# Transposing the gated output by a DMA transfer instead of by TensorE and a ScalarE copy

## What is computed

```
rk = normalise(x per head);  wk = rk one step later;  v = x Wv^T
gate = sigmoid(x Wg^T);  beta = sigmoid(x Wb^T)
for t:  err = (v_t - wk_t S) * beta_t;  S += wk_t err^T;  o_t = (rk_t S) * gate_t
attn = o Wo^T
x = x + layernorm(attn(layernorm(x)))
x = x + layernorm(ffn(layernorm(x)))       # ffn: inputs clipped, weights rounded to -1, 0, 1
```

## Time and profile before

| | |
|---|---|
| median of 3 runs | 2561.44 us (2545.59 to 2561.95) |
| profiled execution | 2552.82 us, span 2551.1 us |
| PE busy | 2161.4 us (85%) |
| PE weight loads busy | 1350.0 us (53%) |
| DVE busy | 2239.5 us (88%) |
| ACT busy | 1699.0 us (67%) |
| POOL busy | 1731.3 us (68%) |
| mean granted TensorE clock | 0.947 of full |
| DMA | 215.50 MB, mean 84 GB/s |

### The profile page before, as it was taken

The page is one execution under the profiler, slowest core; times in us unless marked ns, Lnnn a source line. Parts: engine busy times, 40 slices in busy tenths (PEclk is TensorE's granted clock), DMA queues, the critical chain, the costliest instruction groups (busy, mean ns, idle before and its releaser), DMA issues. The chain is left out here.

```text
span 2551.1 us, 146840 instructions
## 1 busy us (share of the span) xinstructions
PE 2161.4 (85%) x61989; PEld 1350.0 (53%) x61989; DVE 2239.5 (88%) x6603; ACT 1699.0 (67%) x3372; POOL 1731.3 (68%) x2841
## 2 busy tenths in 40 slices
PE   1679999999999999999999989999998747777776
PEld 1356555556555565555655555556655524434442
DVE  4599999999999999999999999999999837777875
ACT  2667777777777777777777777777774335555554
POOL 1556777767777776777777767776775335777777
PEclk7789999999999999999999999999999868888888
DMA  2112222222222222222222222222222124565554
GB/s 79 51 46 63 71 79 76 75 71 72 78 72 78 72 75 72 75 78 71 75 76 78 72 71 78 77 74 71 73 66 62 53 95 146 152 162 153 153 139 99
DMA packets 132137, 215.50 MB, mean 84 GB/s; under 512 B 31352, under 2 KB 31360, under 8 KB 131488
## 3 DMA queue, kind: packets, MB, share of 16 engines
q1 hardware_dynamic: 131488, 206.20, 28.4%
HBM read 104.40 MB, written 67.11 MB: 67 GB/s over the span
## 5 line engine op out<-in xcount | busy, mean ns | idle before, releaser
L740 DVE TENSOR_TENSOR ps_elim<-ps_elim,sys 128x30 f32<-128x30 f32 (+14 forms) x1920 | 543.4, 326 | 0.8
L748 DVE TENSOR_TENSOR sys<-sys,ps_elim 128x30 f32<-128x30 f32 (+14 forms) x1920 | 534.4, 316 | 1.0
L893 PE MATMUL ps_v<-wv,xt 128*128 128x512 f16 x1536 | 433.5, 391 | 34.7 <-DMA kbd<-kt 20.5
L893 PE MATMUL ps_y<-wo,ot 128*128 128x512 f16 x1536 | 404.3, 387 | 12.4 <-DVE x L811 10.1
L1293 PE MATMUL ps_f<-wq,f_xq 128*128 128x512 f16 x1024 | 281.6, 426 | 102.1 <-ACT f_yn L1169 97.5
L920 PEld LDWEIGHTS ps_chain<-rhs,t_t 32*32 32x32 f32 x16384 | 263.1, 144 | 127.0 <-issue 121.7
L543 POOL TENSOR_TENSOR o_g<-pred,gate 128x512 f32<-128x512 f32 x128 | 134.3, 1049 | 286.1 <-DVE pred L827 286.1
L920 PE MATMUL ps_chain<-rhs,t_t 32*32 32x32 f32 x16384 | 294.5, 218 | 20.2 <-issue 12.8
L620 ACT ACTIVATE z<-x,z_sc 128x512 f32<-128x512 f32 x128 | 104.1, 814 | 265.4 <-POOL z_sc L519 265.4
L528 POOL TENSOR_TENSOR m_t<-gram,b_mask 128x512 f32<-128x512 f32 x128 | 164.3, 1283 | 147.7 <-ACT gram L627 141.7
L914 PEld LDWEIGHTS ps_chain<-state,key_t 32*32 32x32 f32 x16384 | 174.5, 105 | 158.2 <-issue 156.4
(11 more groups left out here) (155 smaller groups left out, 5157.7 us busy)
## 6 DMA issues: line engine op xcount, KB each, us to landing
x_in<-in_L_attn_x SPq DMA_DIRECT2D x128, 256.0 KB
kbd<-kt SPq DMA_DIRECT2D x512, 64.0 KB
x_res<-in_L_attn_x SPq DMA_DIRECT2D x128, 256.0 KB
x_scratch<-x SPq DMA_DIRECT2D x128, 256.0 KB, 6.4
f_x<-x_scratch SPq DMA_DIRECT2D x32, 1024.0 KB, 7.6
out<-f_res SPq DMA_DIRECT2D x128, 256.0 KB, 3.9
gate<-gates SPq DMA_DIRECT2D x128, 7.9 KB
gate<-gates SPq DMA_DIRECT2D x128, 0.2 KB
```

Of the source, the lines that this page charges most:

```text
L740: dve.tensor_tensor(tmp, factors(r, c, first, end)[:, c - first:C - 1 - first, c - first:c - first + 1].to_broadcast(shape), sys[:, r, c:c ...
L748: dve.tensor_tensor(dst, dst, tmp, ALU.add).then_inc(elim_done[r], 1)
L893: last = pe.matmul(out, lhs[:, a, kb, :], weights[:, w, kb, :], start=(i == 0), stop=(i == 3 * KB - 1))
```

## The change

PE's transposes and ACT's copy of `ot` are taken out, and with them the bank `ps_ot` and the semaphores `ot_psum` and `ot_done`. SP issues one transposing transfer per tile instead, from `o_part` to `ot`, between the load of `x_res` and the store of `x1`; it waits for `olo_done` of this tile and for the output matmuls of the tile two before. Whoever waited for the transposes (ACT and POOL before they write `o_part`) or for the copy (PE before the output) now waits for the transfer's semaphore, one per buffer.

```diff
+        OT = 16
+        ot_loaded = [sem(f"ot_loaded{i}") for i in range(2)]
@@ SP's step, after the load of x_res
+                n, l, live = on(base, j, LAG_OUT)
+                if live:
+                    wait(sp, s["olo_done"], n + 1)
+                    wait(sp, s["y_psum"], n - 1)
+                    sp.dma_start_transpose(ot[:, l % 2, :, :, :].rearrange("p a k t -> p (a k) t"),
+                                           o_part[:, l % 2, :, :].rearrange("p a n -> p (a n)")).then_inc(ot_loaded[l % 2], 16)
@@ POOL, LAG_PART (before L534), and ACT, LAG_PART (before L601)
-                    wait(pool, s["ot_psum"], n - 1)
+                    wait(pool, ot_loaded[l % 2], halves(base, j, LAG_PART) * OT)
-                    wait(act, s["ot_psum"], n - 1)
+                    wait(act, ot_loaded[l % 2], halves(base, j, LAG_PART) * OT)
@@ ACT, LAG_OUT
-                    wait(act, s["ot_psum"], n + 1)
-                    wait(act, s["y_psum"], n - 1)
-                    nc.scalar.activation(ot[:, l % 2, :, :, :].rearrange("p a k t -> p (a k t)"), ps_ot[:, :].bitcast(F16),
-                                         ACT.Copy).then_inc(s["ot_done"], 1)
@@ PE, LAG_OUT
-                    wait(pe, s["ot_done"], n)
-                    wait(pe, s["olo_done"], n + 1)
-                    for a in range(2):
-                        for kb in range(KB):
-                            last = pe.transpose(ps_ot[:, :].bitcast(F16)[:, D * a + P * kb:D * a + P * kb + P],
-                                                o_part[:, l % 2, a, P * kb:P * kb + P], k["ident_half"][:, :])
-                    last.then_inc(s["ot_psum"], 1)
@@ PE, before the output matmuls
-                    wait(pe, s["ot_done"], y + 1)
+                    wait(pe, ot_loaded[y_l % 2], halves(base, j, LAG_Y) * OT + OT)
```

More of the change, by code:

```diff
@@ L314, in attention @@
         ps_elim = [bank(f"ps_elim{i}") for i in range(2)]
-        ps_ot, ps_v = bank("ps_ot"), bank("ps_v")
+        ps_v = bank("ps_v")
         ps_gram, ps_chain, ps_s, ps_y = bank("ps_gram"), bank("ps_chain"), bank("ps_s"), bank("ps_y")
@@ L336, in attention @@
             pred_psum rhs_done err_psum err_done s_psum state_done
-            pred_done o_done ohi_done olo_done ot_psum ot_done y_psum
+            pred_done o_done ohi_done olo_done y_psum
             y_var y_veps y_rstd x1_done
@@ L640, in step @@
                     nc.scalar.activation(err[:, :], ps_chain[:, :], ACT.Copy).then_inc(s["err_done"], 1)
-                n, l, live = on(base, j, LAG_OUT)
-                if live:
-                    wait(act, s["ot_psum"], n + 1)
-                    wait(act, s["y_psum"], n - 1)
-                    nc.scalar.activation(ot[:, l % 2, :, :, :].rearrange("p a k t -> p (a k t)"), ps_ot[:, :].bitcast(F16),
-                                         ACT.Copy).then_inc(s["ot_done"], 1)
                 n, l, live = on(base, j, LAG_TURN)
```

## The result

The changed kernel takes 2894.74 us at the median (2877.94 to 2912.13, 4 runs) against 2561.69 us: 1.1315 times as long, interval 1.1232 to 1.1398. The forecast was 2605 us, the range 2505 to 2800. The profiled execution took 2898.19 us, its span is 2896.5 us.

A forecast was written before the change was run, and what follows sets the result against it. DVE was taken as today's bound, PE close behind; with the change SP's chain, 12.78 + 2.46 + 0.25 = 15.49 us, 0.34 over today's step: +41 us in 119 steps, +44 with the end, forecast 2605 us, range 2505 to 2800.

The forecast's parts named there:

- What bounds the kernel: In the long stretch, DVE is the bound with 14.6 us of work in a 15.15 us step, PE right behind.
- SP's chain: SyncE's queue: 12.78 us a step with 2.37 us of slack, growing to 15.49 us with the change.
- the sign of a wrong mechanism: In SP's timeline: SP waiting for kt 1 us or more a step while the kernel is still slower.
- The issue on SP: On SP's queue: one transposing issue a tile, taken as 2.46 us, between 0.61 and 4.9 us.
- The wait for the gates: On SP, the gate transfer behind the new one: 0.25 us more a step, between 0 and 1.15 us.
- The engines' work: On the DMA engines: 0.9 us for each 256 KB, with 2.5 us of issuing giving them time to drain.
- the cost that had no term: On PE: only the removal was counted, at best ending DVE's wait for PE, 0.42 us a step.
- a way to be wrong: On PE: its "issue" waits might grow with the traffic; no size was given.
- The landing: Transfer's arrival in ot: 5.5 us after its issue starts, 0.1 to 0.35 us past DVE's limits.
- Rival 3: DVE stalls in L779 behind ACT's L601 because of a late landing of 6.4 us: 2615 to 2645 us, chance 0.12.
- Rival 2: On SP, the eight blocks are paid one by one, 4.9 us of issue: about 2895 us, chance 0.21.
- Rival 1: SP's slack swallows the issue and freed PE and ACT time shows: about 2525 us, chance 0.27.

The follow-up runs named there:

- the swap: The changed kernel with the transposing transfer and the load of x_res exchanged in SP's order, so it stands right behind kbd: 2589.84 us, ratio 1.0092.
- e6_early: The changed kernel with the transposing transfer moved up in SP's order, in front of kbd: 2593.32 us, ratio 1.0072.
- e2_three: The changed kernel with three buffers of o_part instead of two: 2869.64 us, ratio 1.1237 to the kernel before.
- e12_removed: The changed kernel without any transfer in place of PE's transposes and ACT's copy, ot staying zero: 2564.87 us, ratio 1.0046 to the kernel before.
- e3b_plain_three: The changed kernel with a plain transfer of the same bytes instead of the transposing one, and three buffers of o_part: 2566.65 us, ratio 0.9984.
- e1_beside: The kernel before plus a transposing transfer of the same size to a spare tile, for which only SP waits: 2972.26 us, ratio 1.1644.

## Why the prediction was wrong, step by step

**What bounds the kernel: right.** DVE with PE behind it, and SP's chain with 2.4 us of slack; the swap, which uses the slack up, shows that chain as the bound (0.16 us of wait for `kt` left). There the forecast's mechanism holds, and its time is near, 2605 against 2589.84 us. In the change itself it does not: SP waits 3.0 us a step for `kt`, which the prediction had named as the sign of a wrong mechanism.

**The issue on SP: overstated.** 2.46 us was taken; the median is 1.29 us in the change and 1.27 in the swap, the mean 1.55 and 1.64. Some of the rest came back in other issues: in the swap SP issues for 7.6 us a step in all against 5.5 before. The time hardly depends on size: 1.24 us (median) for half the columns. By the 32 cycles a tile of the Trainium skill's page "DMA: Bandwidth & Descriptors", in its table of sequencer time, half the columns should have cost half; the rows do not agree. The wait for the gates, for which 0.25 us was added, is 6.8 us a step, as before.

**The engines' work: the step that failed.** "so 0.9 us for each 256 KB", and "2.5 us of issuing gives the engines time to drain". A plain transfer's price was put on the transposing one, and nothing was asked about the load ahead of it. By the DMA share the engines' work has grown from 3.9 us a step to 9.1 (0.50 x 18.1), by 5.1 us; by 2.1 us in `e6_early`, where nothing is in front (0.39 x 15.5), and by 0.7 us with the plain transfer (0.30 x 15.6), for which the prediction's price is about right. From first to last packet it lasts 5.07 us, 1.7 where nothing is in front.

**PE: the cost that had no term.** The sum had only gains on PE. That its issue waits could grow with traffic stood last, as a way to be wrong. They grew by 2.3 us a step. They were in the profile before, 0.85 us a step, up to 1.5 us long; asking what feeds the instruction stream would have led to the DMA queue.

**The landing: right in kind, small in size.** 5.5 us was taken, 6.8 is the median. Rival 3's chain, `L601` to `L779`, is in the trace at 1.5 us a step, but it does not add to the starvation: `e2_three` takes it away, and the ratio only goes from 1.1315 to 1.1237.

**Rival 2 has the number by luck.** It gave 2895 us for an issue of 4.9 us. The issue is under a third of that, and SP waits for others. The Trainium skill's page "VectorE: DVE Perf Modes" (The three transpose paths), with 1309 ns a block, warned in the right direction; the blocks don't come in series, though, eight pass in 1.7 us at an idle queue. The Trainium skill's page "Advanced Engine Details and Errata" (X-Bar Transpose) has such transfers as fast as regular ones; the rows here do not agree, with 2.1 us of the engines' work at an idle queue against 0.7 for the plain transfer.

**Rival 1's gain did not exist.** 25 to 50 us were promised for the freed PE and ACT time. `e12_removed` and `e3b_plain_three` put it at nothing, within 0.5%.

What was shown and what was argued: that the transfer makes PE stop is shown by `e1_beside`; that the load in front stretches it, by the swap and by half the load. That the stops go through instruction fetches rests on PE's stops without a semaphore and on how they end, 1.4 us after a fetch record or with the transfer; no run changed the fetches themselves. Why a block whose record is complete takes effect only at the transfer's end is open.

## What to carry to other kernels

This kernel, which is written out, gets its instructions by DMA like its data (477 blocks on queue q8): before adding a transfer, look at PE's "issue" waits and at what one long transfer could do to them. Here the transposing transfer cost about 1% where the queue in front of it was empty or held transfers within SBUF or a store, and 13% right behind a load from HBM, so its place in the queue is worth trying first. Give the buffer that it reads one more copy if an engine waits for the landing. Price the removal by itself first: here the work that was moved off PE had been filling a wait.

## What the hardware showed unexpectedly

- A transposing transfer of 256 KB lasts 1.7 us at an idle queue, 2.3 behind 256 KB within SBUF, 5.1 behind a load of 256 KB from HBM, 3.2 behind half of that load.
- It takes 2.1 us of each DMA engine's time at an idle queue; a plain transfer of the same bytes takes 0.7.
- SP's issue of it takes 1.27 us for 1024 columns, 1.24 for 512, and 3.88 at the median behind the load of `x_in`.
- Behind the load of `x_res`, the 16 KB fetches of PE's instructions start inside it at a fifth of the rate that its share of time gives (19 of 89), and 42 of 51 long stops of PE end within 0.6 us of its last packet.
- Before the change 30 of PE's 37 stops of over 0.8 us end 1.2 to 1.7 us after the record of an instruction block.
- In a standstill of 4 us PE's granted clock fell, and it stayed at 0.50 for about 4 us more.
